# Attention values stored 17 columns wide, and the first operand stack loaded from ScalarE's queue during the projections

## What is computed

```python
x = x + attention_a(layernorm(x)); x = x + ffn(layernorm(x))
x = x + attention_b(layernorm(x)); x = x + ffn(layernorm(x))

q, k, v = (x @ W + b, split into 16 heads of 16 columns)
scores  = q @ k.T / 4, masked below the diagonal (layer a adds a decay term)
ctx     = softmax(scores) @ v
out     = ctx @ Wo + bo
# ffn: 2 shared experts plus the best 6 of 32 routed experts, hidden size 176
```

## Time and profile before

| | |
|---|---|
| median of 3 runs | 3129.2 us (3112.96 to 3131.95) |
| the profiled execution | 3135.2 us, its span 3133.4 us |
| layer 0: last projection on PE ends, first max job, first scores of unit 0 | 110.3, 124.3, 162.1 us |
| layer 1: last projection on PE ends, first scores of unit 0 | 1669.1, 1722.2 us |
| PE, DVE, ACT, POOL busy, of the span | 83%, 66%, 52%, 45% |

### The profile page before, as it was taken

One profiled execution on the slowest core, in us unless ns is written; L12 is line 12 of the kernel. 1 busy time (PEld: TensorE's weight loads), 2 busy tenths in 40 slices (PEclk: granted clock), 3 DMA queues, 4 the chain that ended last, 5 costly groups with the idle time before them and its releaser, 6 DMA issues.

```text
span 3133.4 us, 72452 instructions
## 1 busy us (share of the span) xinstructions
PE 2614.6 (83%) x17832; PEld 1946.6 (62%) x17832; DVE 2075.2 (66%) x4624; ACT 1643.9 (52%) x2861; POOL 1395.5 (45%) x1046
## 2 busy tenths in 40 slices
PE   7699999999973799999385999999998728999992
PEld 5455565555553788888363555655555618888882
DVE  8666676776561687777395666766765517777872
ACT  3245444444411788888331554434444208888882
POOL 3430002314245688888544200023142457888885
PEclk9899999999987999999787999999999869999996
DMA  6975645555665789889859644564557648898988
GB/s 222 230 162 128 144 100 108 143 123 164 198 227 192 137 151 157 153 153 155 175 172 221 137 84 89 100 134 128 121 161 223 231 164 149 153 155 154 155 155 204
DMA packets 317281, 494.55 MB, mean 158 GB/s; under 512 B 55706, under 2 KB 225052, under 8 KB 311772
## 3 DMA queue, kind: packets, MB, share of 16 engines
q1 hardware_dynamic: 224908, 361.85, 43.9%
q0 software_dynamic: 92160, 130.08, 25.1%
HBM read 264.26 MB, written 256.77 MB: 166 GB/s over the span
## 4 chain that ended last, share of the span: by engine, by line
PE 45%; DMA 18%; issue 17%; POOL 6%; DVE 6%; SPq 3%; DVEq 2%; POOLq 1%; ACT 1%; ACTq 1%
PE ps L1576 10%; DMA expert_rows<-x 9%; PE ps L1590 9%; PE ps L1607 8%; DMA expert_sum<-x,route_u 5%; PE ps L1859 5%; PE ps L1877 4%; POOL expert_rows L1464 3%; PE ps L1594 2%; PE ps L1580 2%; SPq L424 2%; POOL expert_sum L1491 1%; DMA split<-rows_scratch 1%; DVE split L1171 1%; POOL split L1414 1%
## 5 line engine op out<-in xcount | busy, mean ns | idle before, releaser
L1282 ACT ACTIVATE work<-ps 128x1024 f32<-128x1024 f32 (+3 forms) x768 | 594.9, 810 | 679.0 <-PE ps L1594 458.1
L1464 POOL DMA_INDIRECT expert_rows<-x x372 | 365.4, 982 | 1272.1 <-DVE x L979 805.6
L1491 POOL DMA_INDIRECT expert_sum<-x,route_u x512 | 825.7, 1613 | 195.7 <-issue 92.5
L817 DVE TENSOR_REDUCE small<-ps 128x1 f32<-128x512 f32 (+3 forms) x1216 | 727.3, 656 | 216.9 <-PE ps L1580 145.1
L1576 PE MATMUL ps<-split 128*128 128x512 f32 (+3 forms) x1536 | 510.6, 408 | 72.3 <-DVE work L845 32.2
L1590 PE MATMUL ps<-split 128*128 128x512 f32 (+3 forms) x1536 | 501.6, 406 | 28.1 <-DMA split<-split 27.0
L1859 PE MATMUL ps<-split 128*88 128x256 f32 x3072 | 417.0, 285 | 86.2 <-DVE split L1171 50.4
L1859 PEld LDWEIGHTS ps<-split 128*88 128x88 f32 x3072 | 362.9, 155 | 134.9 <-issue 132.9
L1576 PEld LDWEIGHTS ps<-split 128*128 128x128 f32 x1536 | 275.0, 199 | 269.7 <-DVE small L817 144.8
L1877 PE MATMUL ps<-split 97*128 97x256 f32 x3072 | 408.8, 282 | 2.4 <-DVE split L1186 2.2
L1877 PEld LDWEIGHTS ps<-split 97*128 97x128 f32 x3072 | 384.7, 189 | 3.0 <-issue 2.9
(11 more groups left out here) (179 smaller groups left out, 3152.2 us busy)
## 6 DMA issues: line engine op xcount, KB each, us to landing
x<-expert_rows SPq DMA_DIRECT2D x256, 320.0 KB
split<-qks_scratch SPq DMA_DIRECT2D x192, 256.0 KB
qks_scratch<-split SPq DMA_DIRECT2D x64, 512.0 KB, 4.5
expert_rows<-in_pads SPq DMA_DIRECT2D x65, 320.0 KB, 16.0
v_scratch<-work SPq DMA_DIRECT2D x64, 256.0 KB, 4.3
split<-v_scratch SPq DMA_DIRECT2D x32, 512.0 KB, 14.3
xT_scratch<-split SPq DMA_DIRECT2D x16, 1024.0 KB
split<-xT_scratch SPq DMA_DIRECT2D x16, 1024.0 KB
```

Source lines behind the costliest of these rows:

```text
L817: v.tensor_reduce(cols[:, heads[0]:heads[0] + len(heads), i], ps[:, task_bank(n), 0:w * len(heads)].rearrange("p (h k) -> p h k", k=w), AX ...
L1282: c.activation(pexp[:, (s % 2) * 2 + h, :, BLK - w:], ps[:, 2 * h:2 * h + 2, BLK - w:], ACT.Exp).then_inc(s_pe, 1)
L1464: pool.indirect_dma_start(rows, bass.IndirectOffsetOnAxis(ap=posu[b][:, t * 8 + k:t * 8 + k + 1], axis=0), row_tile(b, t // TPB, t % TPB), ...
L1491: pool.indirect_dma_start(acc[r], bass.IndirectOffsetOnAxis(ap=idx[:, j, k:k + 1], axis=0), ye[:, r3, k, :], None, compute_op=ALU.add).the ...
```

## The change

1. The staging tile, the scratch tensor in HBM and the value buffers hold 17 columns a head, without gaps: a block's v goes out in runs of 4 tokens x 4 heads x 17 columns = 1088 bytes, and a unit's values come back in one run of 2176 bytes a partition. DVE fills the staging tile with four copies of 256 columns instead of two of 512. The product with the values still takes 32 columns of weights, from starts that are multiples of 17; the last 15 belong to the next head.
2. Both halves of stack 0 are zeroed by POOL, after it has finished block 3; DVE's part is gone.
3. The rows and loads of stack 0 are issued by ACT, between its work on block 4 and block 5. The extra two rows (L443) are not loaded a second time for this first turn.
4. SP stores all eight blocks without a break, then loads the rows and operands of stack 1 and goes to the barrier.
5. After the barrier `load_neg_max(0)` stands ahead of the wait for the landed stores.

```diff
-    vds = nc.dram_tensor("v_scratch", (NU, P, NQB, HG * 32), F32, kind="Internal").ap()
+    vds = nc.dram_tensor("v_scratch", (NU, P, 2, TPB * HG * VW), F32, kind="Internal").ap()
...
-                with sp.Fori(0, B - 1) as b:
+                with sp.Fori(0, B) as b:
                     for r in range(2):
                         store_block(b, r)
-
-                sp.wait_ge(s_rowc, 16)
-                load_rows(0)
-                for r in range(2):
-                    sp.wait_ge(s_pd[r], (L * B + 1) * 64 + 64)
-                load_stack(0, 0)
-                store_block(B - 1, 0)
                 load_rows(1)
                 load_stack(1, 1)
-                store_block(B - 1, 1)
                 phase_end(sp, L, 0)
...
-                for r in range(2):
-                    sp.wait_ge(s_pd[r], (L * B + B) * 64 + 64)
-                    sp.wait_ge(s_vd[r], (L * B + B) * 64 + 64)
...
                 load_neg_max(0)
+                for r in range(2):
+                    sp.wait_ge(s_pd[r], (L * B + B) * 64 + 64)
+                    sp.wait_ge(s_vd[r], (L * B + B) * 64 + 64)
                 load_values(0, 0)
...
-                v.memset(vst[:, :, :, :, HD:32], 1.0)
+                v.memset(vst.rearrange("p r u t h c -> p (r u t h) c")[:, :, HD:VW], 1.0)
...
-                    for f in range(2):
-                        last = v.tensor_copy(vst[:, r, :, 8 * f:8 * f + 8, 0:HD],
-                                             ps[:, 6 + f, :].rearrange("p (t h c) -> p t h c", t=TPB, h=8))
+                    for u in range(HG):
+                        last = v.tensor_copy(vst[:, r, u, :, :, 0:HD],
+                                             ps[:, 6 + u // 2, :].rearrange("p (t h c) -> p t h c", t=TPB, h=8)
+                                             [:, :, u % 2 * HG:u % 2 * HG + HG, :])
...
-                dve.wait_ge(s_pj, (L * NBLK + 4) * 6)
-                v.memset(stack32[64:P, 0, 0], 0.0).then_inc(s_zq, 1)
...
+                def first_stack():
+                    act.wait_ge(s_rowc, 16)
+                    act.wait_ge(s_zero[0], L * 2 + 2)
+                    for r in range(2):
+                        act.wait_ge(s_pd[r], (L * B + 1) * 64 + 64)
+                    apart(act)
+                    for o in range(2):
+                        act.dma_start(stack32[48:SROWS, 0, o], rows_scratch[ds(L, 1), o].unsqueeze(2)
+                                      .broadcast_to([1, SROWS - 48, HG, T]).rearrange("o s h t -> (o s) h t")
+                                      ).then_inc(s_stk[0] if o else s_rows[0], 16)
+                    for o in range(2):
+                        for g, s in enumerate(((0, 0, 1), (0, 1, 0))[o]):
+                            act.dma_start(stack32[16 * g:16 * g + 16, 0, o],
+                                          qks[o, s, 0].rearrange("(h w) t -> w h t", h=HG)).then_inc(s_stk[0], 16)
...
-                for b in range(B - 1):
+                for b in range(B - 2):
                     for r in range(2):
                         qkv_block(b, r, True)
+                qkv_block(B - 2, 0, True)
+                first_stack()
+                qkv_block(B - 2, 1, True)
...
+                for o in range(2):
+                    p.memset(stack32[64:P, 0, o], 0.0).then_inc(s_zero[0], 1)
+                pool.wait_ge(s_zero[0], L * 2 + 2)
+                apart(pool)
+                for b in range(B - 2, B):
+                    for r in range(2):
+                        qk_lo(b, r)
...
-                        last = mm(ps[32 * h:32 * h + 32, 6, BLK - w:], vreg[:, r, kb, h, :],
+                        at = (kb * HG + h) * VW
+                        last = mm(ps[32 * h:32 * h + 32, 6, BLK - w:], vreg[:, r, at:at + 32],
...
                 pe.wait_ge(s_stk[0], stack_count(L, 0, 0))
+                pe.wait_ge(s_rows[0], (L + 1) * 16)
```

More of the change, by code:

```diff
@@ L68 @@
 NQB = T // P
+VCOLS = NQB * HG * (HD + 1)
+VSLOT = VCOLS + 32
 SROWS = 68
+VW = HD + 1
 NPHASE = 4
@@ L193, in build @@
         stack32 = stack.bitcast(F32)
-        vreg = split[:, 24576:27648].bitcast(F32).rearrange("p (r t h c) -> p r t h c", r=3, t=NQB, h=HG)
+        vreg = split[:, 24576:24576 + 3 * VSLOT].bitcast(F32).rearrange("p (r n) -> p r n", r=3)
         wqkv = wreg[:, 0:3072].rearrange("p (m k s n) -> p m k s n", m=3, k=KD, s=2)
@@ L238, in build @@
         fqk = work[:, 0:2048].rearrange("p (r f t) -> p r f t", r=2, f=2)
-        vst = work[:, 2048:6144].rearrange("p (r t h c) -> p r t h c", r=2, t=TPB, h=H)
+        vst = work[:, 2048:2048 + 2 * TPB * H * VW].rearrange("p (r u t h c) -> p r u t h c", r=2, u=HG, t=TPB, h=HG)
         vf = work[:, 6144:8192].rearrange("p (r f t) -> p r f t", r=2, f=2)
@@ L303, in build @@
         s_zero = [sem(f"stack_zeroed{r}") for r in range(3)]
-        s_zq = sem("first_query_stack_zeroed")
         s_vl = [sem(f"values_loaded{r}") for r in range(3)]
@@ L424, in store_block @@
                         sp.dma_start(
-                            vds[b * HG + u, :, r * TPB:(r + 1) * TPB, :],
-                            vst[:, r, :, HG * u:HG * u + HG, :].rearrange("p t h c -> p t (h c)")
+                            vds[b * HG + u, :, r, :],
+                            vst[:, r, u].rearrange("p t h c -> p (t h c)")
                         ).then_inc(s_vd[r], 16)
                 def load_rows(r):
-                    sp.wait_ge(s_zero[r], (L + 1) * (1 if r == 0 else 2))
-                    if r == 0:
-                        sp.wait_ge(s_zq, L + 1)
+                    sp.wait_ge(s_zero[r], (L + 1) * 2)
                     for o in range(2):
@@ L441, in load_stack @@
                                          qks[o, s, u].rearrange("(h w) t -> w h t", h=HG)).then_inc(s_stk[r], 16)
-                    sp.wait_ge(s_rows[r], (L + 1) * 32)
+                    sp.wait_ge(s_rows[r], (L + 1) * (32 if r else 16))
                     sp.dma_start(stack32[66:68, r, 0], rows_scratch[L, 0, 0:2].unsqueeze(1)
@@ L446, in load_values @@
                 def load_values(u, r):
-                    sp.dma_start(vreg[:, r], vds[u].rearrange("p t (h c) -> p t h c", h=HG)).then_inc(s_vl[r], 16)
+                    sp.dma_start(vreg[:, r, 0:VCOLS], vds[u].rearrange("p r n -> p (r n)")).then_inc(s_vl[r], 16)
                 def load_unit(u, r):
@@ L1415, in qk_lo @@
                                             ALU.subtract).then_inc(s_pl, 1)
-                with pool.Fori(0, B - 1) as b:
+                with pool.Fori(0, B - 2) as b:
                     for r in range(2):
@@ L1420, in _ @@
                 pool.wait_ge(s_pj, (L * NBLK + 4) * 6)
-                pool.wait_ge(s_pl, (L * NBLK + 6) * 4 + 4)
+                pool.wait_ge(s_pl, (L * NBLK + 4) * 4 + 4)
                 apart(pool)
-                p.memset(stack32[64:P, 0, 1], 0.0).then_inc(s_zero[0], 1)
-                pool.wait_ge(s_zero[0], L + 1)
-                for r in range(2):
-                    qk_lo(B - 1, r)
+                for o in range(2):
[5 more added lines that the diff above has]
+                        qk_lo(b, r)
                 pool.wait_ge(s_pj, (L + 1) * (NBLK * 6))
```

## The result

The changed kernel took 3109.8 us (median of 8 runs, 3095.3 to 3116.3), the kernel before 3128.4 beside it (8 runs, 3113.0 to 3136.5). The ratio is 0.9934, 95% interval 0.9914 to 0.9955: 18.6 us less, where 33 were forecast. The time lies in the range that was forecast, and the change is under 1%.

A forecast was written before the change was run, and what follows sets the result against it. The end of phase 0 was taken as bound by SP's order of issues and, behind it, transfer time. Saving 16.6 us in each layer, 33 us, takes the profiled 3135.2 to 3102, less 6 for the median: 3096 us, range 3079 to 3120.

The forecast's parts named there:

- ACT's eight issues: ACT issuing stack 0's two rows and six stack transfers after block 4: 4.3 us, stopping PE for 2.2 us.
- Zeroing: POOL zeroing stack 0 after block 3, 6.96 us until 78.5: covered, costing PE 0, with 2 us as other end.
- Slack of two blocks between a store and its next use: End of phase 0: two blocks lie between a store and its buffer's next use, the argument against stores being starved.
- rival B: ACT's queue starves the stores: first max job at 121, scores at 150 to 152, 20 to 24 us saved, some 3107; chance 0.17.
- From max jobs to maxima: End of phase 0, layer 0: from first max job to maxima ready takes 24.9 us, so maxima at 139.2.
- Stack 1 is late next: End of phase 0: stack 1's landing limits next; first scores between 142.6 and 150, taken as 145.5, 16.6 us saved.
- Layer 1 like layer 0: End of phase 0 in layer 1: same parts at the same distances, so 16.6 us saved again.
- Values: 17-wide values: a block's stores take 7.5 us instead of 9.35; DVE's four copies cost 0.4 us once a layer.
- Rival A: End of phase 0: transfers don't limit, computation path decides; 19.5 us saved in layer 0, 3089 in all; chance 0.15.
- Rival C: The barrier only waits for something else, such as stack 1's rows; under 10 us saved, 3122; chance 0.07.
- Rival D: Phase 1 slower: value weights starting at multiples of 68 bytes load slower; 3173 at 25 ns a product; chance 0.06.
- the prediction's own signs of being wrong: First max job after 118, maxima's transfer issued after 145, DVE waiting for block 4's stores, or phase 1 longer.

The follow-up runs named there:

- e6_no_zeroing: The changed kernel without any zeroing of the stacks, score products contracting over the 68 loaded partitions instead of 128; 3542.1 to 3616.0 us beside 3123.3 of before.

## Why the prediction was right and where it was wrong

**What bounds the kernel: right.** The end of phase 0 is transfer time. Two edits that only make transfers shorter, narrow values and spread rows, gave 0.9874 together without moving anything.

**ACT's eight issues: right in size, without effect.** 1.09 + 3.26 = 4.35 us against 4.3. But the evacuation behind them waited 4.95 us for PE, so the 2.2 us priced for them were not paid; the zeroing had stopped PE first. Without the zeroing (`e6_no_zeroing`) PE does stop there for ACT, for 1.69 us.

**Zeroing: wrong, priced 0, with 2 us as the other end.** PE stopped for 3.41 + 1.37 = 4.8 us. The 2.1 us that block 5 takes beyond 8.44 are paid in clock: at 80 to 100 us, after these stops, it was granted at 0.83 where before it was 1.00. The row was there, 5.25 against 1.38 us while POOL subtracts; carrying its 3.9 us over left 0.2 us of cover. But a small operation ahead of it (L719) is held too, which I had not looked for, and in layer 1 that one alone took 6.88 us.

**Slack of two blocks between a store and its next use: wrong.** This was the argument against rival B. Stack 0's load holds the engines (161 GB/s at a share of 0.91, 80 to 100 us) and SP's issues (7.72 us for four), and DVE waits 4.97, 3.15 and 1.67 us for stores. In layer 0 that reaches PE as 0.6 us only; in layer 1 it is 2.87, and the 24 matmuls after it take 8.61 us against 5.87. Both failures together: the last transposes of v end at 117.0, not at 112.5, and the first max job starts at 118.75, not 114.3.

**From max jobs to maxima: right.** 144.2 - 118.75 = 25.5 against 24.9.

**Stack 1 is late next: right, and mis-sized.** The transfer path was put at up to 149.9 and first scores at 150 at its late end, if nothing overlaps; they came at 150.70. I took 145.5, since 245 GB/s moved in a stretch that I read as stores in a stack's shadow. That reading was wrong. Cut finer, the stretch has 146 GB/s at 115 to 119 us and 308 at 123 to 127: a stack's tail and then stores, one after the other. And in the changed kernel, with both under way at 80 to 100 us, 161 GB/s moved; the 358 at 115 to 128 us are stores again, since stack 0's slow stretch had ended near 98 us (after which 257 to 402 GB/s move). Stack 1 was issued only at 127.60, six to seven us later than foreseen, and landed 23 us after that, mostly alone. The errors were to count an overlap that the engines did not give, and to count it for a stack that is issued last and has nothing behind it to overlap with.

**Layer 1 like layer 0: wrong.** 8.2 us saved instead of 16.6. The term that was taken as equal, PE's own time in the projections, grew by 13.0 us in layer 1, against 6.7 in layer 0.

**Values: right.** Engine time per block 7.3 us against 7.5 (a block lasts 10.1 us and not 11, but the 286 GB/s over 11 us are a block's 3.15 MB all the same; the narrow block is 2.65 MB, not 2.63). The short runs were the slow ones: before, at a share of 0.99 to 1.03, a block's stores moved 358 to 387 GB/s at 73 to 78 us, where q and k go out, and 286 to 297 at 78 to 81, where v follows. The four copies took 1.42 against 1.29 us, +0.13 instead of +0.4.

**Rival A** fell with stack 1. **Rival B** is the nearest: its place, its DVE wait and its scores of 150 to 152 are what the trace shows, and its 3107 is nearer to 3109.8 than the forecast's 3096; only its first max job of 121 was too late. **Rival C** did not come: stack 1's rows had landed by 136.7, where SP issues the next of it, ahead of the maxima at 144.2. **Rival D** did not either. Line L1620, the product with the values, reads (ns, minimum, median, maximum):

```profile
L1620 PEld LDWEIGHTS ps<-work,split x3072: 105/108/155, 158.2 to 2369.5; 128*32 128x32 f32 x192
```

108 ns against 109: starts at multiples of 68 bytes cost nothing.

The chances put 0.55 on a gain of 24 to 39 us; it was 18.6. Two of the prediction's own signs of being wrong came: the first max job after 118 (118.75), and DVE waiting for block 4's stores (4.97 us). And the gain has another source than I argued: I put most of it on stack 0 leaving the path, and the runs show that this part gives nothing, while the narrow values, which I had only counted as shorter stores inside the transfer path, give all. That the time lies in the range is to that extent luck: the range was wide enough to hold rival B.

What stays open: what decides whether DVE gets in between short zeroings, and whether another place for the zeroing, clear of DVE's normalising, would make the new order pay. That was not tried.

## What to carry to other kernels

Where the transfer engines are the limit, as here, shortening a transfer paid in either order (0.9936 in the old one, 0.9934 against 1.0019 in the new), and moving one only changed who waits. Price a moved transfer by the stores that it pushes back, however long the moved one itself may take. Price an operation of POOL by what DVE does at the same time, tiny operations too (here 3.42 and 6.88 us instead of 0.2). And change one half at a time: here one run of each half showed that one of them does nothing.

## What was not expected of the hardware

- Contracting over 68 instead of 128 partitions came with a granted clock in phase 1 of 0.76 to 0.82 instead of 0.99 (200 to 480 us) and 0.56 to 0.60 instead of 0.95 (480 to 760 us), and with 13 to 17% more time, in three kernels, with PE as busy as before.
- Sixteen rows written to every third partition instead of to neighbours gave 0.5% on top of the change (0.9888 against 0.9934) and 0.6% on the kernel before. SP pays for it with longer issues, 596 against 426 ns in the median, which here is hidden.
- Four issues on SP took 12.98 us while ACT's queue was loading stack 0, and 2.06 with the narrow values in the changed kernel, where the next four took 7.72.
- Beside the same 32 short zeroings on POOL, DVE's four normalising operations took 8.53 us in layer 0 and 1.67 in layer 1.
